# Strip products in two column tiles of 64 rows, weights in smaller pieces, and decode steps in other places

## The reference, cut to what matters

```python
def reference(x, w1, w2, b2, sparse_mask, qweight, lut4, lut8, bias):   # x (4, 512, 1024), weights (1024, 1024)
    attn = jnp.einsum('ds,td->st', w1, w2) * sparse_mask
    y = jax.nn.gelu(jnp.einsum('bds,st->bdt', x, attn) + b2, approximate=False)
    x = _layernorm(x + y)
    e = jnp.linalg.norm(x, axis=-1)
    w_l = dequant_kbit(qweight, lut4, 4)      # 4 bit planes, a table of 16 per row
    w_h = dequant_kbit(qweight, lut8, 8)      # 8 bit planes, a table of 256 per row
    y = jnp.where((e > 64.0)[..., None], einsum(x, w_h), einsum(x, w_l)) + bias
    return _layernorm(x + y)
```

## Time and profile before

| | |
|---|---|
| median of 3 runs | 297.0 us (296.19 to 297.24) |
| profiled execution | 297.11 us, its span 295.1 us |
| PE matmul busy | 280.9 us (95%), 1835 matmuls |
| PE weight loads busy | 245.2 us (83%) |
| DVE busy | 222.3 us (75%) |
| ACT busy | 196.1 us (66%) |
| POOL busy | 57.0 us (19%) |
| DMA | 49.78 MB, mean 169 GB/s |

### The profile page before, as it was taken

One profiled execution on the slowest core, in us unless ns is written; L12 is line 12 of the kernel. 1 busy time (PEld: TensorE's weight loads), 2 busy tenths in 40 slices (PEclk: granted clock), 3 DMA queues, 4 the chain that ended last, 5 costly groups with the idle time before them and its releaser, 6 DMA issues.

```text
span 295.1 us, 4871 instructions
## 1 busy us (share of the span) xinstructions
PE 280.9 (95%) x1835; PEld 245.2 (83%) x1835; DVE 222.3 (75%) x380; ACT 196.1 (66%) x257; POOL 57.0 (19%) x83
## 2 busy tenths in 40 slices
PE   6999999899999999999999999999999999999990
PEld 2788866667668999999999999999988887887780
DVE  1679999897868977997979686297589778656272
ACT  2866368988999879989989996472457484113110
POOL 4000001533354211221200000001141124262101
PEclk9999999999999999999999999999999999999998
DMA  6999999999999711111111111165088754333423
GB/s 207 400 359 359 376 376 340 242 244 244 207 201 195 147 39 36 56 36 51 40 39 53 38 53 38 51 141 221 16 289 273 244 196 178 113 139 117 171 92 132
DMA packets 28480, 49.78 MB, mean 169 GB/s; under 512 B 2464, under 2 KB 11936, under 8 KB 28448
## 3 DMA queue, kind: packets, MB, share of 16 engines
q1 hardware_dynamic: 23392, 40.53, 39.9%
q0 software_dynamic: 4352, 8.39, 15.8%
q10 hardware_dynamic: 704, 0.46, 0.5%
HBM read 36.79 MB, written 12.58 MB: 167 GB/s over the span
## 4 chain that ended last, share of the span: by engine, by line
PE 69%; ACT 7%; SPq 7%; DVE 7%; issue 5%; DMA 3%; POOLq 0%; POOL 0%; DVEq 0%; ACTq 0%
PE acc L577 17%; PE acc L579 17%; PE acc L578 17%; PE acc L506 4%; DMA w<-in_w2d 3%; PE acc L481 2%; SPq L286 2%; ACT leaf L753 2%; ACT zz L796 2%; PE acc L516 2%; PE acc L482 2%; PE acc L483 2%; DVE leaf L1045 1%; PE acc L560 1%; DVE zz L1087 1%
## 5 line engine op out<-in xcount | busy, mean ns | idle before, releaser
L577 PE MATMUL acc<-lin,zz 128*128 128x256 f32 (+2 forms) x424 | 130.7, 308 | 0.3 <-issue 0.3
L579 PE MATMUL acc<-lin,zz 128*128 128x256 f32 (+2 forms) x424 | 129.9, 306 | 0.0
L578 PE MATMUL acc<-lin,zz 128*128 128x256 f32 (+2 forms) x424 | 129.5, 305 | 0.0
L577 PEld LDWEIGHTS acc<-lin,zz 128*128 128x128 f32 x424 | 80.1, 189 | 4.5 <-issue 0.5
L579 PEld LDWEIGHTS acc<-lin,zz 128*128 128x128 f32 x424 | 80.0, 189 | 4.1
L578 PEld LDWEIGHTS acc<-lin,zz 128*128 128x128 f32 x424 | 80.2, 189 | 3.9
L753 ACT ACTIVATE leaf<-planes,lut,flip 128x1024 f32<-128x1024 uint8 x56 | 67.5, 1237 | 1.3 <-DVE dest L1045 1.3
L1045 DVE COPY_PREDICATED leaf<-planes,leaf 128x1024 f32<-128x1024 uint8 x32 | 43.6, 1364 | 13.9 <-ACT leaf L753 13.2
L864 ACT ACTIVATE junk<-rows,cols 128x1024 bf16<-128x1024 f32 x15 | 17.2, 1147 | 34.1 <-DVE cols L1171 34.1
L1045 DVE COPY_PREDICATED dest<-planes,leaf 128x1024 f32<-128x1024 uint8 x24 | 32.5, 1356 | 3.7 <-ACT leaf L753 2.3
L1533 POOL DMA_DIRECT2D z<-in_xr x16 | 19.4, 1218 | 70.9 <-ACT z L735 69.5
(11 more groups left out here) (115 smaller groups left out, 408.4 us busy)
## 6 DMA issues: line engine op xcount, KB each, us to landing
z<-in_xt SPq DMA_DIRECT2D x16, 512.0 KB, 8.7
z<-in_xr POOLq DMA_DIRECT2D x16, 512.0 KB, 8.5
out_rows<-rows SPq DMA_DIRECT2D x15, 512.0 KB, 3.4
out_rows<-parts SPq DMA_DIRECT2D x32, 128.0 KB, 1.7
rows<-out_rows SPq DMA_DIRECT2D x16, 256.0 KB, 2.8
w<-in_w1d SPq DMA_DIRECT2D x7, 512.0 KB, 9.0
off_band<-in_mask_rest SPq DMA_DIRECT2D x8, 448.0 KB, 4.8
w<-in_w2d SPq DMA_DIRECT2D x3, 584.0 KB, 9.0
```

The source lines that it names most:

```text
L577: nc.tensor.matmul(bank, hi, w_hi, start=k == 0, stop=False)
L578: nc.tensor.matmul(bank, hi, w_lo, start=False, stop=False)
L579: last = nc.tensor.matmul(bank, lo, w_hi, start=False, stop=k == KB - 1)
```

## The change

- Each strip product becomes two, one for the upper 64 rows of the result and one for the lower 64, each with 72 extra columns on one side only: 200 columns each, and in blocks 0 and 7 one of 200 and one of 128. The two write to different halves of the partitions of one bank, and so use different column tiles of the array. The parts of the strip that nobody reads are no longer made.
- The back weights are loaded in pieces of two row blocks, eight pieces of each matrix instead of four, with the second piece of q_low behind the last piece for blocks 4 and 5. TensorE waits for each piece.
- x_hi of the first pair of group 0 is made by ScalarE instead of VectorE.
- Decode steps: 13 instead of 11 before the mask of strip 0, then 1 and 1 and none, 15 in all instead of 17. In the mixing 4 and 2, 3 and 1, 3 and 0, 2 and 0; in the linear stage tile 3 has 2 instead of 1. The sum over all is unchanged.
- Semaphores of the branch that is not taken are shared with others, and the one of the flips becomes a fourth step of the tables'.

The lines that matter:

```diff
--- before.py
+++ after.py
...
+    BACK_ROWS = 2
+    BACK_PIECES = KB // BACK_ROWS
...
-    X_ON_ACT = (1, 3)
+    X_ON_ACT = ((0, 1, 3),) + ((1, 3),) * (GROUPS - 1)
+    X_HI_BEFORE = list(itertools.accumulate((len(pairs) for pairs in X_ON_ACT), initial=0))
+    X_ROUNDED_BEFORE = [PAIRS * g - n for g, n in enumerate(X_HI_BEFORE)]
     DECODE = LEAVES + 3
-    EARLY_STEPS = [11, 1, 1, 1, 1, 2, 0, 0]
-    MIX_STEPS = [(3, 3), (2, 1), (2, 1), (2, 0)]
+    EARLY_STEPS = [13, 1, 1, 0, 0, 0, 0, 0]
+    MIX_STEPS = [(4, 2), (3, 1), (3, 0), (2, 0)]
     MIX_Z = {2: ((0, 0), (0, 1)), 3: ((0, 2), (0, 3))}
...
-    FIRST_STEPS = [2, 2, 2, 1, 1, 2, 1, 2, 1, 2, 2, 2, 2, 2, 2, 2]
+    FIRST_STEPS = [2, 2, 2, 2, 1, 2, 1, 2, 1, 2, 2, 2, 2, 2, 2, 2]
...
             def load_back(n, h):
-                signal = w_loaded[len(ROW_PIECES) + 2 * n + h]
-                rows = slice(h * HALF_BLOCKS, (h + 1) * HALF_BLOCKS)
+                signal = w_loaded[len(ROW_PIECES) + BACK_PIECES * n + h]
+                rows = slice(h * BACK_ROWS, (h + 1) * BACK_ROWS)
...
             load_back(0, 0)
+            load_back(0, 1)
             load_band(0)
+            load_back(0, 2)
+            load_back(0, 3)
             load_q(1)
-            load_back(0, 1)
             load_back(1, 0)
+            load_back(1, 1)
             load_band(1)
             load_x(0, 0)
-            load_back(1, 1)
+            load_back(1, 2)
+            load_back(1, 3)
             load_x(0, 1)
...
             def strip_row(b, d):
-                first, end = strip_of(b)
-                return nc.tensor.matmul(unit_bank(b)[:, places_of(b)], w1[:, d, b * P:(b + 1) * P], w2[:, d, first:end],
-                                        start=d == 0, stop=d == KB - 1)
+                for rows_, low, high in ((slice(0, SIDE), REACH, 0), (slice(SIDE, P), 0, REACH)):
+                    first, end = max(b * P - low, 0), min((b + 1) * P + high, D)
+                    to = unit_bank(b)[rows_, first - b * P + REACH:end - b * P + REACH]
+                    half = w1[:, d, b * P + rows_.start:b * P + rows_.stop]
+                    last = nc.tensor.matmul(to, half, w2[:, d, first:end], start=d == 0, stop=d == KB - 1)
+                return last
...
-                    if d % HALF_BLOCKS == 0:
-                        pe.wait_ge(w_loaded[len(ROW_PIECES) + 2 * n + d // HALF_BLOCKS], 32)
+                    if d % BACK_ROWS == 0:
+                        pe.wait_ge(w_loaded[len(ROW_PIECES) + BACK_PIECES * n + d // BACK_ROWS], 32)
...
                 if b == KB - 1:
+                    make_x_hi(0, 0)
                     make_x_hi(0, 1)
...
             def make_x_lo(g, r):
-                if r in X_ON_ACT:
-                    dve.wait_ge(x_hi_made, len(X_ON_ACT) * g + X_ON_ACT.index(r) + 1)
+                if r in X_ON_ACT[g]:
+                    dve.wait_ge(x_hi_made, X_HI_BEFORE[g] + X_ON_ACT[g].index(r) + 1)
...
```

More of the change, by code:

```diff
@@ L1 @@
+import itertools
 import numpy as np
@@ L209, in by_word @@
             return row.rearrange("p (s w k) -> p k s w", s=BITS, k=KB)
-        w_loaded = [sem(f"w_loaded{n}") for n in range(len(ROW_PIECES) + 4)]
+        w_loaded = [sem(f"w_loaded{n}") for n in range(len(ROW_PIECES) + 2 * BACK_PIECES)]
         band_loaded = [sem(f"band_loaded{s}") for s in range(2)]
@@ L221, in post_ln_block @@
         residual_done = [sem(f"residual_done{r}") for r in range(PAIRS)]
-        warm_made, consts_made, flips_made = (sem(n) for n in ("warm_made", "consts", "flips"))
+        warm_made, consts_made = sem("warm_made"), sem("consts")
         planes_made, leaf_made, merged = sem("planes_made"), sem("leaf_made"), sem("merged")
@@ L249, in post_ln_block @@
                                      "x_loaded", "x_hi", "x_lo", "mixed", "gelu", "residual"))
-        (g_table_loaded, g_table_step, g_decoded, g_rows_summed, g_row_mean, g_centred, g_w_ready, g_turned, g_lin_hi_made,
+        (g_table_loaded, g_table_step, g_decoded, g_w_ready, g_turned, g_lin_hi_made,
          g_lin_lo,
          g_low_rows, g_bits_made, g_compared, g_blended) = (
-             sem(f"g_{n}") for n in ("table", "table_step", "decoded", "rows_summed", "row_mean", "centred", "w_ready", "turned",
+             sem(f"g_{n}") for n in ("table", "table_step", "decoded", "w_ready", "turned",
                                      "lin_hi", "lin_lo", "low_rows", "bits", "compared", "blended"))
@@ L260, in strip_of @@
             return max(b * P - REACH, 0), min((b + 1) * P + REACH, D)
-        def places_of(b):
-            first, end = strip_of(b)
-            return slice(first - b * P + REACH, end - b * P + REACH)
         def blocks_of(b):
@@ L694, in general_turns @@
                     pe.wait_ge(g_lin_lo, before + KB + 1)
-                pe.wait_ge(g_ones_made, 1)
+                pe.wait_ge(ones_made, 3)
                 general_turns(0)
@@ L746, in make_leaf @@
                     if b == 0:
-                        act.wait_ge(flips_made, 1)
+                        act.wait_ge(lut_step, 4)
                     to = dest[:, b % 2, :]
@@ L926, in general_weights @@
                             nc.scalar.activation(dest[:, 0, :], dest[:, 0, :], ACT.Copy,
-                                                 accum_out=row_sum[:, 0:1]).then_inc(g_rows_summed, 1)
-                            act.wait_ge(g_row_mean, c + (before + 1))
+                                                 accum_out=row_sum[:, 0:1]).then_inc(rows_summed, 1)
+                            act.wait_ge(row_mean_made, c + (KB + before + 1))
                             nc.scalar.activation(dest[:, 0, :], dest[:, 0, :], ACT.Identity,
-                                                 bias=neg_row_mean[:, 0:1]).then_inc(g_centred, 1)
+                                                 bias=neg_row_mean[:, 0:1]).then_inc(centred, 1)
                             act.wait_ge(g_turned, c + (before + 1))
@@ L1016, in make_x_lo @@
                     nc.vector.tensor_copy(x_hi[:, 2 * r:2 * r + 2, :], z[:, g, 2 * r:2 * r + 2, :]).then_inc(x_rounded, 1)
-                    dve.wait_ge(x_rounded, (PAIRS - len(X_ON_ACT)) * g + r // 2 + 1)
+                    dve.wait_ge(x_rounded, X_ROUNDED_BEFORE[g] + [n for n in range(PAIRS) if n not in X_ON_ACT[g]].index(r) + 1)
                 nc.vector.tensor_tensor(x_lo[:, 2 * r:2 * r + 2, :], z[:, g, 2 * r:2 * r + 2, :],
@@ L1440, in general_weights @@
                                     g_decoded, 1)
-                            dve.wait_ge(g_centred, c + (before + 1))
+                            dve.wait_ge(centred, c + (KB + before + 1))
                             block_ = by_word(dest[:, 0, :])[:, bass.ds(c + HALF_BLOCKS * half, 1), :, :].rearrange(
@@ L1563, in _ @@
                 pool.wait_ge(g_residual, KB * GROUPS + 1)
-                nc.gpsimd.memset(g_ones[:, :].bitcast(f32), 1.0).then_inc(g_ones_made, 1)
+                nc.gpsimd.memset(g_ones[:, :].bitcast(f32), 1.0).then_inc(ones_made, 1)
                 first = slice(0, 1)
@@ L1590, in general_means @@
                     for b in range(before, before + KB):
-                        pool.wait_ge(g_rows_summed, b + 1)
-                        mean_of_row(row_sum[:, 0:1], neg_row_mean[:, 0:1], g_row_mean)
+                        pool.wait_ge(rows_summed, KB + b + 1)
+                        mean_of_row(row_sum[:, 0:1], neg_row_mean[:, 0:1], row_mean_made)
                 general_means(0)
```

5 lines of the change are left out of this document (2 added, 3 removed).

## The result

The changed kernel takes 298.02 us (median of 16 runs, 296.43 to 299.06) against 296.82 us for the one before in the same comparison (median of 16, 295.98 to 297.48). The ratio is 1.0035 with an interval of 1.0021 to 1.0050: slower, by 1.0 us as the ratio has it (0.6 to 1.5), by 1.2 us as the two medians have it. The forecast was +0.5, and its range holds the time.

A forecast was written before the change was run, and what follows sets the result against it. TensorE's work and the weights' arrival bound the start within half a microsecond, then TensorE paces the mixing. +1.0 (new wait net of gains) - 0.5 (old wait gone) on 297.0 gave 297.5 us; range 294.9 to 299.3.

The forecast's parts named there:

- The strips: Strip products on TensorE before the mixing: 0.35 to 0.47 us each in column tiles, ending at 33.6 to 34.1.
- Rival B: Strip products on TensorE: column tiles do not overlap, all mixing waits, +12.2 to 309.2 us; chance 0.10.
- The last piece: End of the back weights' loading: last piece lands at 32.2 again, with 4 strips left behind it, not 8.
- What is late next: Excess strip, after the strips: waits for xe_raw, starts at 36.3 not 36.88, so only 0.5 to 0.6 us passes.
- The new wait: Group 0 of the mixing: ScalarE's centring waits 1.2 us for VectorE's mean; own(1,0) starts 1.0 us later, at 53.35.
- the closer walk: Start of own(1,4) in the mixing, each queue carried step by step: 0.6 us later than before, instead of 0.3.
- From own(1,4) on: Rest of the kernel after own(1,4): steps level again after tile 3 of the linear stage, delay taken as +0.5 us.
- rival C: TensorE's gap before the last weight piece: its clock falls, some 3 us more, half hidden, 299.0 us; chance 0.03.
- The sum: Whole kernel: +1.0 for the mean's wait net of gains, -0.5 for TensorE's old wait that goes, +0.5 us.

The follow-up runs named there:

- the filler: Changed kernel plus two unread fp32 products on TensorE ahead of the third piece of the last weights: 297.26 us, ratio 1.0007.
- the old steps: Changed kernel with the decode steps back where they were before, 17 ahead of the mixing: 299.13 us, ratio 1.0085.
- tiles alone: Kernel before with only the strips in two column tiles, pieces of four rows and all else as before: 297.89 us, ratio 1.0035.

## Why the prediction was right, and where it was not

**The strips (right).** Foreseen 0.35 to 0.47 us a strip, and the last ending at 33.6 to 34.1. The 128 matmuls from 10.81 give (11.34 - 0.33) / 127 = 0.087 us each, 0.347 a strip, the fast end: two column tiles overlap although each half comes twice in a row. Rival B is out (its end of the strips should read 47.7 us, 10.74 + 37, not 47.9, which changes nothing else). A load of 64 columns takes 137 ns and a step 87, so loads lie beside matmuls although both tiles use all rows. The rule of the Trainium skill ("TensorE: Matmul & The Clock Gate", section "Part 3: Packing small matmuls — row/col tiling") that a weight load overlaps a matmul in flight only when it addresses other rows did not hold here either. What the Trainium skill says in "TensorEngine Tiling (Array Packing)", "Key Properties", that different tiles load and multiply in parallel, agrees with that.

**The last piece (right).** Issued at 24.76, it landed 7.7 us later, at 32.46; foreseen 32.2. Behind it stood the last 4 strips, and the 32 matmuls of 2.92 us, begun at the landing of the piece before it, end at 34.04.

**What is late next (right in kind, the gain too large).** The excess strip starts at 36.53, released by xe_raw; foreseen 36.3, and just outside the 36.2 to 36.4 that I had named as the sign. xe_raw landed 0.25 us later than before. raw_e starts at 38.55 (foreseen 38.3), x_lo(0,3) ends at 43.99 (43.75), so VectorE is 0.25 us ahead of before where I had 0.5. Even this is not shown to come from the strips: the kernel with only the steps moved has raw_e at 38.58 and ends x_lo(0,3) at 44.01, though its excess strip starts at 36.67, behind own(0,1).

**The new wait (right in place and size).** Centring waits 1.11 us (1.2), xe_hi(1) starts at 48.03 and ends at 48.6 (48.3), own(1,0) at 53.66 (53.35): +1.27 instead of +1.0, of which 0.25 is the step above. own(1,4) follows without a wait at 58.41, +0.58 where the closer walk said +0.6. The kernel with only the steps moved shows the same wait (1.09 us) and the same start. This is the cause that is shown.

**From own(1,4) on (wrong).** I wrote that the steps are level again after tile 3 of the linear stage, and took nothing more to be lost. The count of the steps is level there, the time is not. TensorE at the next turn that waits, before and then after:

```profile
134.51 1.16 PE L516 MATMUL acc<-eye,dest 128*128 128x128 f32 x8 [0.24 <-DVE dest L1057]
```

```profile
135.49 1.16 PE L525 MATMUL acc<-eye,dest 128*128 128x128 f32 x8 [0.53 <-DVE dest L1067]
```

This is turn(3), for TURN_IN_FIRST has turn(2) in tile 6 and turn(3) in tile 12; the prediction calls its identity that of block 2, but it is that of block 3. Ahead of the wait the lag is +0.69, behind it +0.98, and +0.96 is what VectorE's last bias shows. The extra leaf of tile 3 leaves ScalarE without the idle time that it had. Its first read of a finished tile (parts) there, before and after:

```profile
107.40 0.39 ACT L846 ACTIVATE parts<-acc 128x258 f32<-128x258 f32 x1 [0.44 <-PE acc L579]
```

```profile
108.50 0.37 ACT L856 ACTIVATE parts<-acc 128x258 f32<-128x258 f32 x1
```

From there ScalarE is 1.1 us late and TensorE about 0.65, and the decode stays about a microsecond late up to the identity of block 3 (135.06 for 134.08). The kernel with only the steps moved shows the same 0.5 us wait, the kernels with steps in the gaps 0.2. So the mis-sized term is the "+0.5" that I took from own(1,4) to the end: it measured +0.96, of which 0.58 was there at own(1,4), 0.3 came at turn(3), and 0.1 grew slowly between them.

**The clock (rival C, far too small a chance).** I gave 0.03 to what then happened in perhaps eight to ten of the 16 runs, if their clocks mean what the profiled execution at 0.985 shows. The reason for the low chance was the 5 us for which the clock stayed up behind the last matmul. That row could not carry it: behind a gap of 2.0 to 2.1 us the clock stayed up in two profiled executions and fell in three. The price is open between two readings: 0.4 us at own(1,0) by the traces, 1.35 us between the medians of the runs at low and at high clock (298.50 and 297.15). The mean clock of a run also counts how soon it falls behind the last matmul. In the profiled execution of whole strips with steps in the gaps that was about 2 us behind it, and this alone gave a mean of 0.991. So runs at 0.988 to 0.991 may or may not have had a fall in the gap, and the grouping is not pure. The two comparisons of the changed kernel, +1.2 us with ten of 16 runs at a low clock and +0.3 us with one of 12, would fit a price, but their intervals overlap. I have no run that takes the clock away alone, for the filler had no fewer low clocks than the changed kernel beside it.

**The sum.** Forecast +0.5; measured +1.0 by the ratio (0.6 to 1.5), +1.2 by the medians. The order of the work gives +0.96 in the traces, and +1.1 (0.6 to 1.7) in the runs with only the steps moved. That is all of it or nearly all; what is left for the clock, 0 to 0.3 us, is not told from none.

## What to carry to other kernels

When an engine's work is made shorter, look first at which landing or wait ends last beside it: here 1.6 us saved on TensorE became 0.25 at most, because a transfer of 256 KB further down a full queue landed no earlier. Before a step is moved from an early stage into a later one, find the smallest operation in it on which another engine waits (here a mean of 0.14 us) and what stands ahead of it there; and place steps in the gaps that both engines have. With these two steps there the kernel was 0.6 to 0.8 us faster than before, where it had been 0.3 to 1.2 us slower, on other chips. A list of steps that is level again in count can still be late in time. A producer that outruns its data leaves gaps, and a TensorE gap of two microseconds can cost clock behind it; whole strips without a gap were as fast as tiles here.

## What the runs showed of the hardware

- The granted clock fell to half behind gaps of 2.0 to 2.1 us in three profiled executions (the changed kernel again, the old steps, tiles alone) and not in two (the result, tiles with steps in the gaps), and behind a gap of 3.36 us in the one that was traced. The fall started 0.1 to 1.3 us after TensorE was busy again, and lasted 3.4 us in all four.
- At half clock the column-tiled matmuls took 4.60 us for 32 instead of 2.92: 1.58 times, as only part of the stretch was at half.
- Column tiles of 64 with fp32 operands overlap fully when issued half by half: 87 ns a matmul at a mean of 191 columns, where 173 ns for 200 is the estimate from the strips of before, one by one.
- The time from VectorE's last bias to the end of the span was 6.8 to 7.7 us over the 13 traces, a spread as large as the effect that was measured.
